# Stage one of a graph kernel: the fill on ScalarE's queue, gathers without pacing, dense rows later, and the matrix of equal sources from TensorE

## The reference

```python
h = max(layernorm(x), 0)
# layer 0
gate = silu(edge_attr @ W1.T + b1) @ W2.T + b2
gate += sum(emb[type[src]] * (emb[type[dst]] @ adaptW.T), -1)
cw   = where(dist < 6, 0.5*(cos(pi*dist/6)+1), 0)
msg  = gate * h[dst] * (cw * node_vec[dst])
agg  = segment_sum(msg, src) / segment_sum(node_vec[dst], src)
x    = x + layernorm(h + agg)*gamma + beta
# layer 1
h    = max(layernorm(x), 0)
h1   = relu(h[src] @ weight1[edge_type] + bias1)
x    = x + relu(segment_sum((h1 @ weight2[edge_type]) * norm, dst) + bias2)
```

## Time and profile before

| | us |
|---|---|
| median of 3 runs (1517.62 to 1532.58) | 1523.17 |
| profiled execution, span from first to last instruction | 1526.4 |
| end of stage one (last accumulate into `agg0` landed) | 743.0 |
| first accumulate into `agg0` | 212.7 |
| VectorE, TensorE, ScalarE, GpSimd busy | 1319.3, 1130.4, 668.1, 1026.1 |

### The profile page before, as it was taken

How to read it: one execution, slowest core, us unless ns; L and a number is a source line. 1 busy time by engine, 2 the same in 40 slices (tenths; PEclk the granted TensorE clock), 3 DMA queues, 4 the chain that set the end, 5 groups by cost and what they waited for, 6 DMA issues and landing times.

```text
span 1526.4 us, 20418 instructions
## 1 busy us (share of the span) xinstructions
PE 1130.4 (74%) x5198; PEld 831.4 (54%) x5198; DVE 1319.3 (86%) x3932; ACT 668.1 (44%) x1627; POOL 1026.1 (67%) x809
## 2 busy tenths in 40 slices
PE   5889899989999899881068888887878887775000
PEld 2767677777777777771035555555555555554000
DVE  6999999999989998980289999998989899888599
ACT  2444444544445444540155555555555555554000
POOL 7655667777877787566667787877777777766000
PEclk9666655655556655655575656655565556666555
DMA  7999986666666656642445666555555555554899
GB/s 225 307 324 327 328 236 157 153 146 143 142 166 149 149 139 143 155 101 11 100 120 143 166 167 156 140 138 137 136 139 127 132 131 138 138 127 81 328 400 398
DMA packets 154391, 268.73 MB, mean 176 GB/s; under 512 B 73818, under 2 KB 90411, under 8 KB 153380
## 3 DMA queue, kind: packets, MB, share of 16 engines
q1 hardware_dynamic: 78228, 223.53, 43.8%
q0 software_dynamic: 68992, 24.64, 18.5%
q10 hardware_dynamic: 7056, 19.27, 3.1%
HBM read 194.33 MB, written 112.55 MB: 201 GB/s over the span
## 4 chain that ended last, share of the span: by engine, by line
PE 34%; DVE 20%; DMA 19%; POOL 12%; issue 10%; ACT 3%; SPq 1%; POOLq 0%; DVEq 0%; ACTq 0%
PE ps_m L572 10%; POOL agg L485 8%; DMA t<-agg,src_all 6%; PE ps_m L661 6%; PE ps_qs L572 6%; DMA lows<-low 4%; PE ps_k L647 3%; DVE same L858 2%; DMA agg<-y,once 2%; DMA agg<-ysq,once 2%; DVE t L1074 2%; DVE x L1070 2%; PE ps_k L559 2%; PE ps_k L560 2%; PE ps_qs L610 1%
## 5 line engine op out<-in xcount | busy, mean ns | idle before, releaser
L521 POOL DMA_INDIRECT agg<-sums,once x196 | 312.7, 1595 | 103.5 <-issue 79.8
L443 POOL DMA_INDIRECT nodes<-in_table,dst_all x196 | 194.9, 995 | 102.2 <-issue 51.7
L512 POOL DMA_INDIRECT t<-agg,src_all x196 | 191.5, 977 | 66.1 <-issue 53.9
L572 PEld LDWEIGHTS ps_m<-msg,same 128*128 128x128 f32 x980 | 200.8, 314 | 29.0 <-issue 29.0
L572 PE MATMUL ps_m<-msg,same 128*128 128x48 f32 x980 | 208.5, 398 | 1.0 <-issue 1.0
L647 PE MATMUL ps_k<-h_t,rw_sb 56*128 56x256 f32 x588 | 122.7, 536 | 114.0 <-ACT hid L742 91.3
L572 PEld LDWEIGHTS ps_qs<-msg,same 128*128 128x128 f32 x980 | 183.6, 289 | 2.1 <-DVE msg L950 2.1
L572 PE MATMUL ps_qs<-msg,same 128*128 128x49 f32 x980 | 180.7, 363 | 2.0 <-DVE msg L950 2.0
L485 POOL DMA_INDIRECT agg<-x,once x84 | 137.4, 1635 | 43.9 <-issue 21.7
L647 PEld LDWEIGHTS ps_k<-h_t,rw_sb 56*128 56x128 f32 x588 | 62.9, 242 | 157.1 <-ACT hid L742 115.2
L559 PE MATMUL ps_k<-types_lo,low_hot 128*128 128x392 bf16 x196 | 95.7, 488 | 52.7 <-DVE low_hot L833 51.0
(11 more groups left out here) (149 smaller groups left out, 2620.2 us busy)
## 6 DMA issues: line engine op xcount, KB each, us to landing
agg<-in_both SPq DMA_DIRECT2D x14, 2758.0 KB, 15.3
t<-agg SPq DMA_DIRECT2D x49, 784.0 KB, 5.3
kept<-kept_out SPq DMA_DIRECT2D x49, 404.0 KB
kept_in<-kept SPq DMA_DIRECT2D x49, 404.0 KB, 3.5
agg<-bias_rows SPq DMA_DIRECT2D x49, 384.0 KB
out<-t ACTq DMA_DIRECT2D x49, 384.0 KB, 5.8
rows<-in_src_rows SPq DMA_DIRECT2D x49, 256.0 KB, 4.2
rows<-in_dst_rows SPq DMA_DIRECT2D x49, 256.0 KB, 3.2
```

The costliest lines, as they stand in the source:

```text
L443: pool.indirect_dma_start(nodes[s][:, t, :], None, table, bass.IndirectOffsetOnAxis(ap=dst_all[:, c:c + 1], axis=0)).then_inc(nodes_in[b % ...
L512: pool.indirect_dma_start(t2[b % T2S][:, t, :], None, wide, bass.IndirectOffsetOnAxis(ap=src_all[:, c:c + 1], axis=0)).then_inc(ends_in[b ...
L521: pool.indirect_dma_start(agg1, bass.IndirectOffsetOnAxis(ap=once1[b % LAG1][:, t:t + 1], axis=0), sums1[b % LAG1][:, t, :], None, compute ...
L572: last = mm(ps[:, t * width:(t + 1) * width], kept_same[:, at:at + P], m[:, v, :], start=(v == t), stop=(v == TILES - 1))
```

## The change

1. The 14 fills are issued on ScalarE's queue, all at the start, after the indices are in.
2. GpSimd gathers blocks 1 to 25 (`PRERUN` = 26, was 32) without waits other than for the ring; later ones two tiles a block as before.
3. Dense rows: the first steps come at block 13 (loads at block 11), and the 49 chunks are spread over blocks 14 to 48, one or two in each (`dense_steps`). Their root (`root_dense`) is split from that of the edges (`estd0`).
4. The matrix `same`: the sources are cut into 32 bits, each +1 or -1 (`key_bits`, `key_signs`, once for four blocks, from `rows` loaded 32 partitions a block). The product of two sources' signs is 32 where they are equal and at most 30 where not. TensorE makes the products (`key_dots`, K = 32) and subtracts 64 in its own tile where the column comes later (`later`); ScalarE evicts with Relu(x - 31) and the count (`same_copy`). `turn` and `turn_once` of block b come in block b + 1.
5. Types are looked up two in one number: the table has 196 columns rather than 392 (`NPK`), and a shift and a mask on four columns pick the right one.
6. The one-hot of the destination's type: TensorE spreads the type (bf16) over the partitions, ScalarE squares its distance to the partition's number and takes Relu(1 - x).
7. `keep_clock` issues 512-column bf16 products into a bank that nobody reads: three at the start of a block, one behind the first two lookups, three inside `sums0`, one behind the last `key_dots`, one behind `h1`, and one behind each `centred`.

Cut to its core, the diff is:

```diff
-PRERUN = FIRST + 2 * STEPS
+PRERUN = 26
...
+def dense_steps():
+    steps = [[] for _ in range(NBLOCK)]
+    steps[DENSE0 - 1] = [(None, 0), (None, 1)]
+    c = 0
+    for b in range(DENSE0, NBLOCK):
+        while c * (NBLOCK - DENSE0) < (b + 1 - DENSE0) * NBLOCK:
+            steps[b].append((c, c + 2 if c + 2 < NBLOCK else None))
+            c += 1
+    assert c == NBLOCK and max(len(s) for s in steps) == 2
+    return steps
+
+
+def rooted_at(steps, b):
+    return [s[0] for s in (steps[b - 1][1:] if b > 0 else []) + (steps[b][0:1] if b < NBLOCK else []) if s[0] is not None]
...
+            def load_keys(k):
+                need(sp, S["signs_done"], k - 1)
+                for q in range(GROUP):
+                    b = min(k * GROUP + q, NBLOCK - 1)
+                    sp.dma_start(rows[k % 2][q * NBITS:(q + 1) * NBITS, :],
+                                 src_rows[b:b + 1, :].to_broadcast([NBITS, BE])).then_inc(keys_in[k % 2], 16)
...
-                if b < FILLS:
-                    sp.dma_start(fill_to[b], fill_from[b]).then_inc(S["wide_set"], 16)
...
+                    load_keys(b // GROUP + 2)
...
                     load_lows(b + 2)
-                    load_xt(b + 2)
...
                     rows_set += 1
-                sp.wait_ge(S["std_done"], b + 1)
...
+                if b == DENSE0 - 3:
+                    load_xt(0)
+                    load_xt(1)
+                store_kept(b)
+                for done, begun in steps[b]:
+                    if begun is not None and begun + 2 < NBLOCK:
+                        load_xt(begun + 2)
...
+            for b in range(1, PRERUN):
                 gather(b)
-            for step in range(STEPS):
-                pool.wait_ge(S["onehot_done"], step + 1)
-                gather(FIRST + 2 * step)
-                pool.wait_ge(S["pc_done"], step + 1)
-                gather(FIRST + 2 * step + 1)
...
+            def keep_clock(ps, n):
+                for _ in range(n):
+                    mm(ps, ident_bf[:, :], spin, start=True, stop=True)
...
+            def key_dots(b, t):
+                at = slice(b % GROUP * NBITS, (b % GROUP + 1) * NBITS)
+                bits = signs[b // GROUP % 2]
+                if t == 0:
+                    pe.wait_ge(S["signs_done"], b // GROUP + 1)
+                need(pe, S["same_done"], b * TILES + (0 if t < 2 else t))
+                mm(ps_dots[t], bits[at, t * P:(t + 1) * P], bits[at, 0:(t + 1) * P], start=True, stop=False)
+                mm(ps_dots[t][:, t * P:(t + 1) * P], ident_bf[:, :], later[:, :], start=False, stop=True).then_inc(S["dots_done"], 1)
 
...
                 lookup(0, t)
-            centred(0)
             for b in range(NBLOCK):
+                keep_clock(ps_idle, 3)
                 if b + 1 < NBLOCK:
                     lookup(b + 1, 0)
                     lookup(b + 1, 1)
-                pe.wait_ge(S["onehot_done"], b + 1)
-                need(pe, S["onehot_t_done"], b)
+                keep_clock(ps_idle, 1)
+                pe.wait_ge(S["zd_done"], b + 1)
+                need(pe, S["apart_done"], b)
                 for t in range(TILES):
...
-                last.then_inc(S["turned_t_done"], 1)
+                    last = mm(ps_t[:, t * P:(t + 1) * P], zd_bf[:, t:t + 1].to_broadcast([P, P]), ident_bf[:, :], start=True, stop=True)
+                last.then_inc(S["zd_wide_done"], 1)
+                key_dots(b, 0)
+                key_dots(b, 1)
...
                     sums0(b - 1)
                 pe.wait_ge(S["onehot_t_done"], b + 1)
...
                 last.then_inc(S["gate_done"], 1)
+                key_dots(b, 3)
+                keep_clock(ps_idle, 1)
                 if b + 1 < NBLOCK:
                     h1(b + 1)
-                    centred(b + 1)
+                    keep_clock(ps_idle, 1)
+                for done, begun in steps[b]:
+                    if begun is not None:
+                        centred(begun)
+                        keep_clock(ps_idle, 1)
...
+            act.wait_ge(S["idx_in"], 32)
+            for f in range(FILLS):
+                act.dma_start(fill_to[f], fill_from[f]).then_inc(S["wide_set"], 16)
             act.wait_ge(S["pool_set"], POOL_SET)
...
+            def same_copy(b, t):
+                act.wait_ge(S["dots_done"], b * TILES + max(t + 1, 2))
+                if t == 0:
+                    need(act, S["sums_done"], b - 1)
+                    need(act, S["turned_done"], b)
+                n = P * (t + 1)
+                A(same[b % 2][:, place(t):place(t) + n], ps_dots[t], ACT.Relu, bias=1.0 - NBITS,
+                  accum_out=ahead[:, t:t + 1]).then_inc(S["same_done"], 1)
...
+                act.wait_ge(S["zd_wide_done"], b + 1)
+                A(apart[:, :], ps_t[0:NTYPE, :], ACT.Square, bias=minus_type[:, :]).then_inc(S["apart_done"], 1)
+                act.wait_ge(S["apart_done"], b + 1)
                 need(act, S["q_done"], b)
-                nc.scalar.copy(onehot_t[:, :], ps_t[0:NTYPE, :]).then_inc(S["onehot_t_done"], 1)
+                A(onehot_t[:, :], apart[:, :], ACT.Relu, scale=-1.0, bias=1.0).then_inc(S["onehot_t_done"], 1)
+                same_copy(b, 0)
+                same_copy(b, 1)
                 if b > 0:
                     sums0_copy(b - 1)
                 act.wait_ge(S["var_e_done"], b + 1)
-                act.wait_ge(S["var_d_done"], b + 1)
...
+                A(estd0[:, :], evar0[:, :], ACT.Sqrt, bias=eps[:, :], scale=1.0 / H).then_inc(S["std_done"], 1)
+                for c in rooted_at(steps, b):
+                    root_dense(c)
+                same_copy(b, 2)
+                same_copy(b, 3)
                 if b + 1 < NBLOCK:
                     gate_hidden(b + 1)
-                    hidden(b + 1)
+                for done, begun in steps[b]:
+                    if begun is not None:
+                        hidden(begun)
...
+            V.scalar_tensor_tensor(out=types_two[:, :, :], in0=of_two[:, :, 1, :], scalar=float(P), in1=of_two[:, :, 0, :],
+                                   op0=ALU.mult, op1=ALU.add).then_inc(S["types_set"], 1)
+            dve.wait_ge(S["types_set"], 1)
+            V.tensor_scalar(types_lo[:, :, :].rearrange("p k n -> p (k n)").bitcast(U16),
...
             def type_of(b, t):
                 c = b * TILES + t
-                dve.wait_ge(S["low_done"], c + 1)
-                V.scalar_tensor_tensor(out=junk_l[:, t * NHI:(t + 1) * NHI], in0=iota_hi[:, :], scalar=hi_all[:, c:c + 1], in1=ps_l[t % 2],
+                dve.wait_ge(S["low_done"], c + 2 - t % 2)
+                V.scalar_tensor_tensor(out=junk_l[:, t * NPK:(t + 1) * NPK], in0=iota_hi[:, :], scalar=hi_all[:, c:c + 1], in1=ps_l[t % 2],
                                        op0=ALU.is_equal, op1=ALU.mult, accum_out=zs_all[:, c:c + 1]).then_inc(S["zsel_done"], 1)
...
+            def key_bits(k):
+                dve.wait_ge(keys_in[k % 2], 16 * GROUP * uses(k, 2))
+                V.tensor_scalar(rows[k % 2][:, :], rows[k % 2][:, :], bit_of[:, :], 1, ALU.logical_shift_right,
+                                ALU.bitwise_and).then_inc(S["bits_done"], 1)
+
+            def key_signs(k):
+                dve.wait_ge(S["bits_done"], k + 1)
+                need(dve, S["dots_done"], GROUP * TILES * (k - 1))
+                V.tensor_scalar(signs[k % 2][:, :], rows[k % 2][:, :], 2.0, -1.0, ALU.mult, ALU.add).then_inc(S["signs_done"], 1)
...
+            def turn(b):
+                dve.wait_ge(S["same_done"], TILES * (b + 1))
+                V.scalar_tensor_tensor(out=turned[:, :], in0=ahead[:, :], scalar=1.0, in1=turn0_all[:, b * TILES:(b + 1) * TILES],
+                                       op0=ALU.is_gt, op1=ALU.mult).then_inc(S["turned_done"], 1)
...
                 dve.wait_ge(nodes_in[b % ARRIVE], 16 * TILES * uses(b, ARRIVE))
-                need(dve, S["turned_t_done"], b)
-                V.tensor_tensor(onehot[:, :, :], each(iota_type[:, :], TILES),
-                                node[:, :, H + 1:H + 2].bitcast(I32).to_broadcast([P, TILES, NTYPE]),
-                                ALU.is_equal).then_inc(S["onehot_done"], 1)
+                need(dve, S["zd_wide_done"], b)
+                V.tensor_copy(zd_bf[:, :], node[:, :, H + 1:H + 2].bitcast(I32).rearrange("p t o -> p (t o)")).then_inc(S["zd_done"], 1)
                 V.tensor_reduce(xsum[:, :], node[:, :, 0:H], AX_X, ALU.add).then_inc(S["xsum_done"], 1)
-                dve.wait_ge(rows_in[s], 16 * uses(b, 2))
-                need(dve, S["sums_done"], b - 1)
-                same_up_to(b, src_all, ahead, 0, 2)
-                same_up_to(b, src_all, ahead, 2, 3)
+                if b % GROUP == 2 and b // GROUP + 1 < GROUPS:
...
+                if b % GROUP == 3 and b // GROUP + 1 < GROUPS:
+                    key_signs(b // GROUP + 1)
                 dve.wait_ge(S["xsum_done"], b + 1)
                 need(dve, S["ecsq_done"], b)
```

202 lines of the change are left out of this document (140 added, 62 removed).

## The result

The changed kernel takes **1677.71 us** (median of 4 runs, 1670.14 to 1711.53) against 1520.39 of the kernel before beside it: a ratio of 1.0973, 95% interval 1.0910 to 1.1035. The forecast was 1488 us, the range 1443 to 1545. The profiled execution's span is 1668.1 us, 141.7 more than before; the medians differ by 157. Each ratio here is to the kernel before in the same job and, but for e1, leaves disturbed runs out, so it need not be the quotient of two medians, and e15's trace is of a disturbed run.

What follows compares the result with a forecast made beforehand. GpSimd's accumulates were taken to end stage one at 743.0 us; the change would bring GpSimd's path to 701 and the loop to 699, with disturbance 708, 35 earlier: 1523 - 35 = 1488 us, range 1443 to 1545.

Steps and rivals of the forecast that it cites:

- What bounds the kernel before: Stage one: GpSimd's row of accumulates ends it at 743.0 us; the TensorE, VectorE and ScalarE loop ends some 50 us earlier.
- Gathers: GpSimd before its accumulates: 104 gathers issue in 130 us; slowed by the fill, accumulates start at 171 us, at best 137.
- the sum: End of stage one: GpSimd's path 701 us, loop 699, some 7 us of mutual disturbance: 708 us, 35 earlier.
- The loads of SyncE's queue: Start of stage one: small loads compete with the fill, landed at about 115 us; block 0's `once` at about 130 us.
- GpSimd's start: First accumulate of stage one: 171 us, once the gathers delayed by the fill let GpSimd go on.
- Light blocks: Stage one's first 14 blocks, without dense rows: 10.0 us each at full clock.
- Dense blocks: Stage one's 34 later blocks in the sum, with dense rows: VectorE's 11.2 us plus hand-overs, 12.0 us each.
- hand-overs: Waits between engines in a block with dense rows: added to VectorE's 11.2 us to make 12.0.
- Rival 3: Stage one's loop: clock stays about 0.6, TensorE bounds every block, 14.0 and 16.3 us; 1681 us, or 1581 with harmless fill; chance 0.14.
- Its rule: Rival 3 decides once the loop ends later than GpSimd: a mean above 12.0 us a block if it starts at 130.
- ScalarE's accumulator reads: ScalarE per block, with four added evictions: each read has bounds of 0 to 0.3 us, 0.1 taken.

Runs made afterwards that it cites:

- e1: Changed kernel with the fill issued again on SyncE's queue, one part per block in the first 14 blocks: 1680 us, ratio 1.102.
- e15: Kernel before with packed lookup and idle matmuls, three parts of the fill a block from SyncE, 26 blocks of gathers ahead: 1563 us, ratio 1.009.
- e17: Kernel before without the accumulate of each block's last of four tiles in stage one: 1491 us, ratio 0.974.
- e18: Kernel before with packed lookup and idle matmuls, without the accumulate of each block's last tile in stage one: 1435 us, ratio 0.939.
- e7: Kernel before with the gathers of blocks 1 to 25 issued without a pause: 1640 us, ratio 1.069.
- e6: Changed kernel with GpSimd's gathers paced by the blocks, fill still whole on ScalarE's queue: 1723 us, ratio 1.123.
- e11: Changed kernel with the fill on SyncE and gathers paced by `zd` and ScalarE's copy of the sums, four at a time: 1546 us, ratio 1.016.
- e12: As e11, with dense rows from block 4 instead of block 14: 1544 us, ratio 1.018.
- e2: Changed kernel with `keep_clock` issuing nothing, fill still on ScalarE's queue: 1806 us, ratio 1.180.

## Why the prediction was wrong

**What bounds the kernel before** was read rightly: GpSimd's row of accumulates ends stage one (e17, e18), the loop of blocks ends before it.

**Gathers: a term put at nothing.** "104 gathers x (0.94 + 0.31 us)" priced what the gathers cost GpSimd, and nothing for what they do to the others. Without a pause they hold TensorE, VectorE and ScalarE in the first blocks: the last accumulate comes 105.8 us later in e7. Neither the sum nor a rival had this. In the changed kernel the delay by the fill covers it: with paced gathers the first `once` comes only 6 us earlier (e6). e1, undoing the fill's move, uncovers it, and stage one ends 10 us earlier, no more. Undoing both (e11) gives back 1.097 - 1.016 = 0.081 of 1520, 123 us.

**The loads of SyncE's queue: too short by 32 us.** The mechanism was right, and the upper end was the right one to take: the constants at 136.2 us. "`once` for block 0 at about 130" was 32 us too early; the fill was through at 136 and not at 115, and a first block had to follow. 318 GB/s, not the 366 that 108 us stand for, was what the DMA engines gave. GpSimd's start, 171, was 188.1.

**Light blocks:** 10.0 forecast, 10.95 measured, at a clock of 0.97. The step was right; over twelve blocks it is 11 us short.

**Dense blocks: the step that failed and cost most.** The prediction took VectorE's 11.2 us plus hand-overs, 12.0 us, "with the clock held at 2.4 GHz most of the time". It was 15.9 us at a clock of 0.73. VectorE's work was sized well (398.6 us in 36 blocks, 11.1 each), and so was TensorE's (20.1 at half clock with 1.4 dense steps; a block with one step shows 18.6, and 10.7 at full clock). Two things were wrong. The clock did not hold: it fell in the blocks with two dense steps and stayed down in the next, so that these took 17.1 us, bound by TensorE. And the hand-overs of a block with two steps, priced at 0.8 us like all others, are over 2: such blocks take 15.4 us and more even at a clock of 0.8 to 1.0, with VectorE busy 13.3. With one step and a full clock the block is near the forecast (12.5 us, and 11.2 in e12). That the clock falls because TensorE waits there is read from the order of events at 480 to 487 us and from e12; no run took the wait away alone.

The sum, then: 32 us for the start, 11 for the light blocks and 144 for the dense ones (two of the 36 had been forecast at 10), less 15 of a shorter tail (15.3 us from the last `once` to stage two, where the forecast had 30 in all), lead from 708 us to the 880.9 measured.

**Rival 3** came nearest: TensorE the bound of every dense block, 16.3 us, 1681 us. I gave it 0.14. That its time is so close is luck: light blocks at 14.0 (10.95 measured; 16.9 at half clock comes to 13.6 at 0.62, so even that sum is a little high) and a loop that starts at 130 (161.7) cancel in part, its end of stage one is 20 us late (901 against 880.9), and it has every block bound by TensorE, which those with two steps are not. Its rule, that a loop above 12.0 us a block ends stage one, held. I read the Trainium skill's rule ("TensorE: Matmul & The Clock Gate", What's actually happening), that the throttled clock is the default and activity releases it, as speaking against rival 3. e2 agrees with the default: without the idle matmuls TensorE stays at 1.2 GHz all through stage one. The rule gives no number of idle matmuls that is enough. Ten were enough in the light blocks (0.97) and in e12's row of blocks with one dense step (0.96), and not where every second or third block has two, nor beside the fill in e12.

**ScalarE's accumulator reads** were taken at 0.1 us and are 0.195; the evictions are 0.43 in the mean. What they cost in time was not tried.
